# The masked key blocks of two attention stages: from GpSimd, out of a copy, to ScalarE, head by head

## The reference

```python
gating = softmax(x @ W_gate.T)
idx = argmax(gating); indicator = one_hot(idx); top1_val = max(gating)
q, k, v = split(x @ W_qkv.T, 3)
k_shared = einsum('bth,bthd->btd', indicator, k)
v_shared = einsum('bth,bthd->btd', indicator * top1_val, v)
att = einsum('bhqd,bkd->bhqk', q, k_shared) / sqrt(16)   # causal mask
y   = einsum('bhqk,bkd->bhqd', softmax(att), v_shared)
```

```python
q = qdq(x) @ qdq(wq).T + bq
k, v = split(cond @ wkv.T + bkv, 2)
attn = softmax(einsum('bnhd,bmhd->bhnm', q, k) / sqrt(16))
o = einsum('bhnm,bmhd->bnhd', attn, v)
out = qdq(o) @ qdq(wp).T + bp
```

## Time and profile before

| what | value |
|---|---|
| time, median of 3 runs (lowest, highest) | 996.8 us (995.38, 997.8) |
| span of the profiled execution, first to last instruction | 990.1 us |
| time of the profiled execution itself | not recorded beside its span; the median of the runs is 6.7 us above the span |
| PE busy | 662.3 us, 67% |
| DVE busy | 542.9 us, 55% |
| ACT busy | 266.9 us, 27%, 500 instructions |
| POOL busy | 249.9 us, 25%, 222 instructions |
| mean granted TensorE clock | 0.819 of full speed |

### The profile page before, as it was taken

The page is one execution under the profiler, slowest core; times in us unless marked ns, Lnnn a source line. Parts: engine busy times, 40 slices in busy tenths (PEclk is TensorE's granted clock), DMA queues, the critical chain, the costliest instruction groups (busy, mean ns, idle before and its releaser), DMA issues.

```text
span 990.1 us, 10881 instructions
## 1 busy us (share of the span) xinstructions
PE 662.3 (67%) x3643; PEld 419.3 (42%) x3644; DVE 542.9 (55%) x1043; ACT 266.9 (27%) x500; POOL 249.9 (25%) x222
## 2 busy tenths in 40 slices
PE   1002988866873206878772899665059999999980
PEld 1002344643552101544432466544036666666650
DVE  5877686686877877878985533354301222222213
ACT  1600233223330110755572323141011211212110
POOL 5242222247704054034456000100410000000006
PEclk9555998778776555999996899895579999999995
DMA  6100000020040142343120000596410100000004
GB/s 219 47 0 11 1 2 1 2 53 1 14 88 0 46 126 92 99 122 128 51 67 32 1 1 1 217 429 265 161 53 22 33 21 26 26 26 27 17 22 127
DMA packets 39372, 66.19 MB, mean 67 GB/s; under 512 B 6116, under 2 KB 35428, under 8 KB 36964
## 3 DMA queue, kind: packets, MB, share of 16 engines
q1 hardware_dynamic: 30272, 53.88, 16.3%
q10 hardware_dynamic: 7520, 7.54, 2.4%
q0 software_dynamic: 1536, 4.20, 1.3%
HBM read 47.54 MB, written 17.76 MB: 66 GB/s over the span
## 4 chain that ended last, share of the span: by engine, by line
PE 48%; DVE 24%; POOL 10%; issue 9%; DMA 5%; ACT 3%; SPq 1%; POOLq 0%; ACTq 0%; DVEq 0%
PE bank L1582 14%; PE bank L1603 7%; DVE XN L336 5%; PE bank L1254 4%; DVE region L1054 3%; PE bank L1273 3%; PE bank L519 2%; PE bank L915 2%; PE bank L1593 2%; PE bank L493 2%; DMA channel_maxima<-region 2%; PE bank L1715 2%; PE bank L422 2%; POOL slot_rows L1419 1%; POOL region L1426 1%
## 5 line engine op out<-in xcount | busy, mean ns | idle before, releaser
L1582 PE MATMUL bank<-region,wide 128*128 x368 | 143.7, 544 | 0.3 <-issue 0.3
L1497 DVE TENSOR_TENSOR wide<-wide,bank 128x448 f32<-128x448 f32 x46 | 28.6, 621 | 144.0 <-ACT wide L1536 144.0
L1582 PEld LDWEIGHTS bank<-region,wide 128*128 128x128 f32 x368 | 68.8, 192 | 61.5 <-issue 61.3
L1054 DVE TENSOR_REDUCE region<-bank 128x2 f32<-128x512 f32 x128 | 81.6, 683 | 23.0 <-PE bank L915 21.6
L915 PE MATMUL bank<-region 128*128 128x256 bf16 x256 | 57.4, 317 | 40.1 <-DMA region<-region 26.5
L978 ACT ACTIVATE region<-bank 128x1024 f32<-128x1024 f32 x64 | 65.6, 1024 | 56.6 <-PE bank L939 51.7
L1426 POOL DMA_INDIRECT region<-slot_results,pos x16 | 15.2, 948 | 247.6 <-DMA slot_results<-wide 243.0
L1603 PE MATMUL bank<-region,XN 128*128 x322 | 73.4, 380 | 1.2 <-DVE wide L1510 1.2
L1603 PEld LDWEIGHTS bank<-region,XN 128*128 128x128 f32 x322 | 59.5, 190 | 9.3 <-issue 2.1
L1715 PE MATMUL bank<-ident,XN 128*128 128x128 f32 x96 | 22.4, 423 | 58.3 <-DVE XN L336 47.7
L336 DVE TENSOR_SCALAR XN<-X,meanvar,rstd 128x256 f32<-128x256 f32 x64 | 49.4, 842 | 17.2 <-POOL rstd L341 17.2
(11 more groups left out here) (272 smaller groups left out, 1232.0 us busy)
## 6 DMA issues: line engine op xcount, KB each, us to landing
region<-in_L_ffn_experts_dram SPq DMA_DIRECT2D x8, 2688.0 KB, 19.5
region<-ctx_parts SPq DMA_DIRECT2D x24, 192.0 KB
region<-norm_parts SPq DMA_DIRECT2D x8, 576.0 KB
channel_values<-wide ACTq DMA_DIRECT2D x8, 512.0 KB, 5.8
slot_rows<-wide SPq DMA_DIRECT2D x1, 2944.0 KB, 24.2
wide<-slot_rows SPq DMA_DIRECT2D x23, 128.0 KB, 2.0
slot_results<-wide SPq DMA_DIRECT2D x23, 128.0 KB, 1.7
ctx_parts<-region SPq DMA_DIRECT2D x40, 64.0 KB, 2.1
```

Of the source, the lines that this page charges most:

```text
L1054: e.tensor_reduce(nmax[i % 2][:, at_:at_ + KC], ps(u).rearrange("p (c n) -> p c n", c=KC), AX.X, ALU.max, negate=True).then_inc(s_chan["ma ...
L1582: last = e.matmul(bank[hf][:, 512 * gu:512 * gu + hw], xbT[par][:, P * c:P * c + P], region[:, bass.ds(off + (2 * gu + c) * I8 + hw * hf, ...
```

## The change

GpSimd no longer builds key blocks in either stage. ScalarE's `key_T` does it, with one activation for each head: a copy of 128 by 128 whose scale is the head's column of `headmask`, so 8 instructions per tile in the first stage, read straight from the transposed keys in PSUM (the copy `kTs` and its semaphore go), and 16 per tile in the second, read from KT. In the first stage the function stands where the copy stood in ScalarE's order. In the second stage it is new to ScalarE and is put last in each step, with lag 0: value_blocks(t-2), probs(t-1), probs_T(t-2), key_T(t). PE's waits on `key_T_ready` become waits on `key_blocks`.

```diff
@@ pool_attention
-            def kbd(i):
-                if i >= 2:
-                    e.wait_ge(s_att["scores_made"], NT * s + i - 1)
-                for c in range(1 if s == 0 else KC):
-                    src = kTs if s == 0 else KT[:, c, P * i:P * i + P]
-                    last = e.tensor_tensor(KBD[i % 2][c], src.unsqueeze(1).broadcast_to([P, HC, P]),
-                                           headmask.unsqueeze(2).broadcast_to([P, HC, P]), ALU.mult)
-                last.then_inc(s_att["key_blocks"], 1)
-
             if s == 0:
-                for t in range(NT + 1):
+                for t in range(NT):
+                    e.wait_ge(s_att["kv_selected"], t + 1)
                     if t >= 1:
-                        e.wait_ge(s_att["key_T_ready"], t)
-                        kbd(t - 1)
-                    if t < NT:
-                        e.wait_ge(s_att["kv_selected"], t + 1)
-                        if t >= 1:
-                            e.wait_ge(s_att["key_T_in_psum"], t)
-                        e.tensor_copy(krep, ...).then_inc(s_att["key_repeated"], 1)
+                        e.wait_ge(s_att["key_T_in_psum"], t)
+                    e.tensor_copy(krep, ...).then_inc(s_att["key_repeated"], 1)
             else:
                 for i in range(NT):
-                    e.wait_ge(s_att["k_ready"], KC * (1 + i // 4))
-                    kbd(i)
                     e.wait_ge(s_att["v_copied"], i + 2 - i % 2)
@@ pe_attention: before the value projection of the second stage
-                e.wait_ge(s_att["key_T_ready"], NT)
@@ pe_attention, key_value(i), i >= 2
-                    e.wait_ge(s_att["key_T_ready"], i - 1)
+                    e.wait_ge(s_att["key_blocks"], i - 1)
@@ pe_attention, values(i), first stage
-                    e.wait_ge(s_att["key_T_ready"], min(i + 3, NT))
+                    e.wait_ge(s_att["key_blocks"], min(i + 3, NT))
@@ act_attention
             def key_T(i):
-                e.wait_ge(s_att["key_T_in_psum"], i + 1)
-                if i >= 1:
-                    e.wait_ge(s_att["key_blocks"], NT * s + i)
-                e.activation(kTs, ps(4 + i % 2, 320, 320 + P), ACT.Copy).then_inc(s_att["key_T_ready"], 1)
+                if s == 0:
+                    e.wait_ge(s_att["key_T_in_psum"], i + 1)
+                else:
+                    e.wait_ge(s_att["k_ready"], KC * (1 + i // 4))
+                if i >= 2:
+                    e.wait_ge(s_att["scores_made"], NT * s + i - 1)
+                if i == 0:
+                    e.wait_ge(s_att["consts"], 4)
+                for c in range(1 if s == 0 else KC):
+                    src = ps(4 + i % 2, 320, 320 + P) if s == 0 else KT[:, c, P * i:P * i + P]
+                    for h in range(HC):
+                        last = e.activation(KBD[i % 2][c][:, h, :], src, ACT.Copy, scale=headmask[:, h:h + 1])
+                last.then_inc(s_att["key_blocks"], 1)
@@
             for t in range(NT + 5):
-                for f, lag in ((key_T, 1), (value_blocks, 2 + L), (probs, 1 + L), (probs_T, 2 + L)):
-                    if 0 <= t - lag < NT and not (s == 1 and f is key_T):
+                for f, lag in ((key_T, 1),) * (1 - s) + ((value_blocks, 2 + L), (probs, 1 + L), (probs_T, 2 + L)) + ((key_T, 0),) * s:
+                    if 0 <= t - lag < NT:
                         f(t - lag)
```

More of the change, by code:

```diff
@@ L185, in program @@
         krep = carve(HC, HD)
-        kTs = carve(P)
         headmask = carve(HC)
@@ L380, in pool_attention @@
         def pool_attention(e, ch, s):
-            def kbd(i):
-                if i >= 2:
-                    e.wait_ge(s_att["scores_made"], NT * s + i - 1)
-                for c in range(1 if s == 0 else KC):
-                    src = kTs if s == 0 else KT[:, c, P * i:P * i + P]
-                    last = e.tensor_tensor(KBD[i % 2][c], src.unsqueeze(1).broadcast_to([P, HC, P]),
-                                           headmask.unsqueeze(2).broadcast_to([P, HC, P]), ALU.mult)
-                last.then_inc(s_att["key_blocks"], 1)
             if s == 0:
-                for t in range(NT + 1):
+                for t in range(NT):
+                    e.wait_ge(s_att["kv_selected"], t + 1)
                     if t >= 1:
-                        e.wait_ge(s_att["key_T_ready"], t)
-                        kbd(t - 1)
-                    if t < NT:
-                        e.wait_ge(s_att["kv_selected"], t + 1)
-                        if t >= 1:
-                            e.wait_ge(s_att["key_T_in_psum"], t)
-                        e.tensor_copy(krep, SEL[:, t, 0:HD].unsqueeze(1).broadcast_to([P, HC, HD])).then_inc(s_att["key_repeated"], 1)
+                        e.wait_ge(s_att["key_T_in_psum"], t)
+                    e.tensor_copy(krep, SEL[:, t, 0:HD].unsqueeze(1).broadcast_to([P, HC, HD])).then_inc(s_att["key_repeated"], 1)
             else:
                 for i in range(NT):
-                    e.wait_ge(s_att["k_ready"], KC * (1 + i // 4))
-                    kbd(i)
                     e.wait_ge(s_att["v_copied"], i + 2 - i % 2)
```

## The result

| | before | changed |
|---|---|---|
| median of 6 runs (lowest, highest) | 995.21 us (993.51, 997.8) | 1034.82 us (1033.07, 1042.26) |
| span of the profiled execution | 990.1 us | 1040.0 us |
| ScalarE busy, GpSimd busy | 266.9, 249.9 us | 319.0, 204.7 us |

The ratio is 1.041, 95% interval 1.0377 to 1.0444: slower by 39.6 us. The forecast was 1043, slower by 46. The profiled executions lie 49.9 us apart, because the changed kernel's was the longest of its six; its own time was 1042.26, 2.3 above its span. Ratios in this document leave out an execution that lies over 1.5% above the fastest of its kernel; that concerns one version alone, two of its six.

The account below looks back on a forecast made before the run. First stage: bound by a ring from krep through PE and VectorE, without key blocks; second: GpSimd's work stretches VectorE's instructions and PE idles. First stage 0, ahead 0, loop +43.4, tail +2.5: +46 on 996.8, 1043 us; range 1020 to 1064.

Parts of the forecast that it names:

- The chain: Second-stage loop: scores, shift, probs, probs_T copy and sixteen activations run end to end per tile, 10.9 to 14.0 us.
- The price: ScalarE, one small activation with a column as scale: about 0.30 us per head in the second stage, 0.27 in the first.
- The sum 0.31 + 0.07 - 0.09: Second-stage activation price: 0.31 us for the copy, plus 0.07 for the operand column, minus 0.09 for overlap; about 0.30.
- rival B: No overlap between a second-stage tile's sixteen activations, 0.40 us each: +12.8 us, 1057, or 1062 at low clock; chance 0.17.
- The first stage: First attention stage: ScalarE's eight activations per tile replace the copy and GpSimd's blocks; value 0, bounds -0.5 to +3 us.
- The tight third tile: First stage's tightest turn: ScalarE done with gate_sum and its accumulator at 125.9, against VectorE's reading at 126.06.
- The three microseconds of slack: First stage: GpSimd's key block is done at 149.12, PE reaches the scores reading it only after 152.35.
- Ahead of the loop: Second stage before its loop: L336 -2.2 and L628 -1.8 us, then 4.95 us for key_T(0); gain and loss cancel.
- The loop: Second stage from scores(0) to scores(7): 90.4 us, four turns of five at the lower clock; +43.4 us.
- The tail: Second stage from scores(7) to the end of the last values: 17.2 us becomes 20, +2.5 us.
- The frame: Whole kernel: profiled span 990.1 becomes 1036; runs' median 6.7 above the span, so 996.8 + 46 = 1043 us.
- Rival D: Second stage: freeing VectorE from GpSimd outweighs ScalarE's blocks if hidden, VectorE at most 6.4 us a tile; 983 us, chance 0.03.

Follow-up runs that it names:

- The reordered kernel: Full change, but in the second stage each ScalarE step begins with tile t's key blocks instead of ending with them; ratio to before 1.0011, median 997.7 us.

## Why the prediction was right

**The chain, right.** It was named as the term that decides, and shown three ways: the order alone takes the loss away (1.0011), a block longer by 3.0 us lengthens the common turns by 2.6 to 3.0 and the second stage by 20.8, and the trace has scores 0.05 us behind the last activation.

**The price, right.** 0.30 us per head were taken; 4.77 us for sixteen are 0.292 from start to start, at a length of 0.388. The sum 0.31 + 0.07 - 0.09 gives 0.29 and was rounded up; 4.95 for a tile with its hand-over was 0.13 too high for that (4.82 from the first activation to the scores). From PSUM the sum gives 0.26, and 0.27 was taken; the step is 0.25. The choice between the overlapping L1775 and the separate L594 went to the right row, and rival B's price of 0.40 without overlap is refuted for activations on all 128 partitions.

The estimate from the Trainium skill (page "ScalarE: Activation LUTs", section "What ACT_TABLE_LOAD costs") was 0.29 per head, and the trace agrees from SBUF, in length and in step. From PSUM the length agrees (0.385) but the step of 0.25 does not, and the measurement decides.

**The first stage, right.** 0 was forecast, 0.9983 (0.9961 to 1.0005) measured. The tight third tile held: gate_sum's accumulator was read out by 124.98, and VectorE's L652, which follows, started at 125.40. The three microseconds of slack were read from a full turn; in the third tile there is less than one, the block being done at 123.13 and PE's first matmul of the scores (L489) starting at 123.71 before, 122.38 and 123.04 (L471) in the changed kernel. That was enough.

**Ahead of the loop, right in kind, small in size.** -4.0 was forecast; L336 and L628 gave 2.3 + 1.8 = 4.1. The trace has -5.5; the other 1.4 lie in PE's query projection, which ran at a higher clock. Scores(0) came 34.6 us after the norm's root, where it was 35.5 before and 36.2 in the forecast: gain and loss nearly cancel, as said.

**The loop, right in sum, in part by luck.** 90.4 us were forecast from scores(0) to scores(7), 89.9 were measured. With all turns at the low level it was to be 11.8, 12.3 and five turns of 14.0, at full clock 10.4 and six of 10.9; a mean of the two was taken, four to one. Measured were 12.0, 12.5, 12.5, 12.5, 13.9, 13.9, 12.6. The clock did not choose one level for a whole turn: scores always began at the lower one (3.68 us), and in three of the five turns with values it came back in time for the transposes (1.09 at 260.38). That kind of turn, 12.5 us, the forecast did not have, and none came out at 10.9. The mean of two kinds of loop that did not occur came within half a microsecond of the one that did.

**The tail, too large.** +2.5 was forecast, and it is 0.1: from scores(7) to the end of the last values 17.2 us before, 17.3 after.

**The frame, off.** The forecast started from 996.8, the median of three executions; that of all six is 995.2. And 6.7 us were taken as what lies around the span, though in all executions here the time is 1.7 to 3.6 us above it: the profiled execution before was one of the shorter ones. In medians the loss is 39.6 us and not 46. The traces' second stages say 42.7 up to the start of the last values and 41.4 up to their end, since those ran at the higher clock in the changed kernel (1.94 us instead of 3.20). The 2 us between lie within what the clock does to a single trace, and no run here settles them.

**Rival D** named its own condition, that the queue ran the blocks elsewhere. The reordered kernel does, and comes to 1.0011 and not to D's 983, since ScalarE's own 7.41 us then set the turn, and not VectorE's 6.4, with which D had reckoned. Only with half the blocks back on GpSimd and the first tiles prebuilt does the time reach 984 and 988. Of that, keeping GpSimd's blocks out of VectorE's way ahead of the loop was measured alone, at about 5 us (0.9954).

## What to carry to other kernels

When work moves to an in-order engine, ask first what stands ahead of it in that queue and what it waits for: last in the step, behind an instruction that depends on its own last product, it lays the whole loop end to end and a double buffer buys nothing. The same work at the head of the step cost nothing here, and half of it on each engine, with the first tiles built in idle time, made the kernel about 1% faster than it had been. Work taken off GpSimd pays on VectorE, if VectorE's instructions beside it were stretched: look for groups of one line whose members differ in length.

## What the runs showed of the hardware

- ScalarE, 128 by 128 with an operand column as its scale: 0.388 us long from SBUF, 0.385 from PSUM, but from start to start 0.292 from SBUF (4.77 for 16) and 0.25 from PSUM (2.18 for 8). The forecast had the step from PSUM shorter because it had the length shorter; in fact the lengths are alike. With 64 columns from SBUF it is 0.34 long and steps by 0.24 (7.77 for 32).
- TensorE's granted clock stayed at 1.00 for 49 us with rests of 1.26 us in each 10.77 us turn. With rests of 5.4 to 6.9 us in turns of 12.5 to 13.9 it was 0.65 over the same window.
- The same first stage took 96.2 to 105.0 us in different executions: mostly by how many turns take 12.25 to 12.5 instead of 9.35 us, at a clock of 0.72. In the shortest, the values of its last two tiles also ran at full clock, 1.82 instead of 3.20 us. One trace of each kernel can't tell such luck from an effect of the change; the lengths of the stages, side by side, show in which stage the two differ.
